# Linear attention with a mixing layer and a gated FFN: q's and k's fp16 parts by one cast and one subtraction, the clamp folded into the product, and new orders of all stages

## The reference

```
x = inv(I - circulant(ricker(width, damp))) @ x        # over channels
t = x as 1024 tokens of 128
a = layernorm(t)
Q, K = elu(a @ Wq.T) + 1, elu(a @ Wk.T) + 1            # 8 heads of 16
V    = a @ Wv.T
S, z = cumsum over tokens of K (x) V, of K
t = t + ((Q . S) / max(Q . z, 1e-6)) @ Wout.T
z = layernorm(t)
g = mean over tokens of gate(z)                        # 8 gates per batch
t = t + layernorm_affine(z + FFN(z)), FFN's weights merged by g
out = t back in x's layout
```

## Time and profile before

| | |
|---|---|
| median of 3 runs | 771.26 us (769.69 to 775.61) |
| profiled execution | 771.21 us, span 769.4 us |
| PE busy | 699.8 us (91%) |
| DVE busy | 670.8 us (87%) |
| ACT busy | 648.9 us (84%) |
| POOL busy | 534.8 us (70%) |
| DMA queue q1 | 82.0 MB, 46.6% of 16 engines' span |
| mean granted clock of PE | 0.968 |

### The profile page before, as it was taken

One profiled execution on the slowest core, in us unless ns is written; L12 is line 12 of the kernel. 1 busy time (PEld: TensorE's weight loads), 2 busy tenths in 40 slices (PEclk: granted clock), 3 DMA queues, 4 the chain that ended last, 5 costly groups with the idle time before them and its releaser, 6 DMA issues. The chain is left out here.

```text
span 769.4 us, 41594 instructions
## 1 busy us (share of the span) xinstructions
PE 699.8 (91%) x13218; PEld 549.2 (71%) x13218; DVE 670.8 (87%) x2615; ACT 648.9 (84%) x1860; POOL 534.8 (70%) x1167
## 2 busy tenths in 40 slices
PE   4897989999999999999999999768999998999993
PEld 2566767777777777777777777656777787777772
DVE  5697889999999999999999999657889877898983
ACT  3687989999999999999999999645888885888883
POOL 3788889999999999999999999420333331333333
PEclk9999989999999999999999999699999999999997
DMA  5558575665666666666665664510122220222221
GB/s 145 112 94 145 104 131 125 132 141 133 129 147 136 134 140 142 138 136 140 134 145 131 139 144 99 82 37 23 43 84 82 82 69 15 84 82 82 82 82 68
DMA packets 202343, 82.60 MB, mean 107 GB/s; under 512 B 176076, under 2 KB 189551, under 8 KB 202232
## 3 DMA queue, kind: packets, MB, share of 16 engines
q1 hardware_dynamic: 202296, 81.99, 46.6%
HBM read 22.69 MB, written 17.30 MB: 52 GB/s over the span
## 5 line engine op out<-in xcount | busy, mean ns | idle before, releaser
L874 DVE SCALAR_TENSOR_TENSOR scores_lo<-p_a,scores_hi 128x512 f16<-128x512 f32 x256 | 175.8, 687 | 7.1 <-ACT scores_hi L760 3.4
L760 ACT ACTIVATE scores_hi<-p_a 128x512 f16<-128x512 f32 x256 | 161.7, 641 | 11.0 <-PE p_a L601 10.7
L979 POOL CAST qk_parts<-qk_f 128x256 f16<-128x256 f32 x256 | 108.8, 427 | 6.3 <-issue 4.3
L1414 POOL TENSOR_TENSOR ffn_rstd_shift<-ffn_rstd_shift,consts 128x4 f32<-128x4 f32 x32 | 36.6, 1142 | 108.8 <-DVE ffn_rstd_shift L1372 108.8
L989 POOL TENSOR_TENSOR qk_parts<-qk_f,qk_parts 128x128 f16<-128x128 f32 x256 | 103.9, 426 | 0.9
L1350 DVE TENSOR_TENSOR h_lo<-h_f,h_hi 128x512 f16<-128x512 f32 x128 | 95.7, 786 | 0.9 <-ACT h_hi L1252 0.9
L1196 PE MATMUL psb<-merged_W_of_batch,h_hi 128*128 128x128 f16 x512 | 94.1, 220 | 2.2 <-DVE h_lo L1350 1.6
L1241 ACT ACTIVATE h_f<-psb,merged_b_of_batch 128x512 f32<-128x512 f32 x128 | 87.0, 710 | 10.3 <-PE psb L1177 8.6
L1197 PE MATMUL psb<-merged_W_of_batch,h_hi 128*128 128x128 f16 x512 | 93.7, 219 | 0.0
L1198 PE MATMUL psb<-merged_W_of_batch,h_lo 128*128 128x128 f16 x512 | 93.7, 219 | 0.0
L618 PE MATMUL p_o<-v_parts,scores_hi 128*128 128x17 f16 x1024 | 90.4, 171 | 2.0 <-issue 0.2
(11 more groups left out here) (215 smaller groups left out, 2859.4 us busy)
## 6 DMA issues: line engine op xcount, KB each, us to landing
x_f<-in_x SPq DMA_DIRECT2D x32, 256.0 KB, 3.1
t_rows<-t SPq DMA_DIRECT2D x64, 128.0 KB, 2.4
t_back<-t_rows SPq DMA_DIRECT2D x32, 256.0 KB, 2.6
out<-out_tile SPq DMA_DIRECT2D x32, 256.0 KB, 2.0
tv_share<-in_L_ffn_tv_W SPq DMA_DIRECT2D x32, 128.0 KB
qkT_parts<-qk_parts SPq DMA_TRANSPOSE x128, 3.1
zT_hi_lo<-z_parts SPq DMA_TRANSPOSE x128, 2.3
merged_W<-in_L_ffn_W SPq DMA_DIRECT2D x2, 256.0 KB, 4.1
```

Source lines behind the costliest of these rows:

```text
L760: nc.scalar.activation(ah[:, t % 2, cols], p_a[:, cols], ACT.Relu).then_inc(ahi_ready[eo], 1)
L874: nc.vector.scalar_tensor_tensor(al[:, t % 2, cols], p_a[:, cols], 0.0, ah[:, t % 2, cols], ALU.max, ALU.subtract).then_inc(alo_ready[eo], 1)
L979: nc.gpsimd.tensor_copy(dst, src.unsqueeze(2).broadcast_to([P, NH, 2, DH])).then_inc(done, 1)
```

## The change

Three things:

- q's and k's hi parts are written by one cast of 512 elements per partition (each value of q and k twice) and their lo parts by one subtraction of 256, in place of two casts and two subtractions. For that k's columns are laid out as lo, hi, hi, 0 and q's as hi, hi, lo, 0, so that one access pattern with a step of 528 columns reaches both; the tile gets 32 columns more per buffered tile (PKW = 1056). The semaphores qhi_ready and khi_ready become qkhi_ready.
- The clamp of the denominators (a tensor_scalar on DVE) goes. invert takes the reciprocal of the sum in PSUM, and divide becomes one scalar_tensor_tensor: min(1/den, 1/(1e-6 VS)) times the numerators.
- All five order tables are new, in order and in skews. Among the skews: project 0 to 1, gate 13 to 15, turn_z 10 to 14, z_hi 10 to 11, z_lo 10 to 12, normalise 10 to 11, gate_relu 14 to 15, rsqrt1 1 to 0, load_x 3 to 4, invert 5 to 6.

```diff
+PKW = 2 * (NH * 4 * DH + DH)
...
-TENSOR_ORDER = [("state", 3), ("scores", 4), ("turn_out", 6), ("conv", 0), ("values", 5), ("out_project", 6),
-                ("project", 0), ("gate", 13)]
+TENSOR_ORDER = [("gate", 15), ("state", 3), ("project", 1), ("scores", 4), ("conv", 0), ("turn_out", 6),
+                ("values", 5), ("out_project", 6)]
...
-SYNC_ORDER = [("turn_z", 10), ("turn", 2), ("load_x", 3), ("load_tv", 3), ("store", 8)]
+SYNC_ORDER = [("turn_z", 14), ("turn", 2), ("load_x", 4), ("load_tv", 3), ("store", 8)]
...
-                    def denominator(b, t):
+                    def invert(b, t):
                         n = TILES * b + t
                         dve.wait_ge(av_done, n + 1)
-                        nc.vector.tensor_scalar(dn[:, t % 2, 0, :], num[:, :, DH], 1e-6 * VS, None, ALU.max)\
-                            .then_inc(den1, 1)
...
+                        nc.vector.reciprocal(dn[:, t % 2, :], num[:, :, DH]).then_inc(den2, 1)
...
-                        nc.vector.tensor_tensor(o_[:, t % 2, :].rearrange("p (h i) -> p h i", i=DH), num[:, :, 0:DH],
-                                                dn[:, t % 2, 1, :].unsqueeze(2).broadcast_to([P, NH, DH]), ALU.mult)\
+                        nc.vector.scalar_tensor_tensor(o_[:, t % 2, :].rearrange("p (h i) -> p h i", i=DH),
+                                                       dn[:, t % 2, :].unsqueeze(2).broadcast_to([P, NH, DH]),
+                                                       1.0 / (1e-6 * VS), num[:, :, 0:DH], ALU.min, ALU.mult)\
                             .then_inc(o_ready, 1)
...
+                    def parts_of(tile, first, w_step, width):
+
+                        return bass.AP(pkw[:, :, :].tensor, PKW * tile + first,
+                                       [[4 * PKW, P], [w_step, 2], [4 * DH, NH], [1, width]])
...
+                        src = qk[:, t % 4, :].rearrange("p (g i) -> p g i", i=DH)
+                        nc.gpsimd.tensor_copy(parts_of(t % 4, 0, NH * 4 * DH + DH, 2 * DH),
+                                              src.unsqueeze(2).broadcast_to([P, 2 * NH, 2, DH])).then_inc(qkhi_ready, 1)
...
-                        for w in range(2):
-                            src = qk[:, t % 4, w * C:(w + 1) * C].rearrange("p (h i) -> p h i", i=DH)
-                            lo = pk[:, t % 4, w, :, (1 + w) * DH:(2 + w) * DH]
-                            last = nc.gpsimd.tensor_tensor(lo, src, pk[:, t % 4, w, :, 0:DH], ALU.subtract)
-                        last.then_inc(lo_ready, 1)
+                        pool.wait_ge(qkhi_ready, n + 1)
+                        nc.gpsimd.tensor_tensor(parts_of(t % 4, 2 * DH, NH * 4 * DH - 2 * DH, DH),
+                                                qk[:, t % 4, :].rearrange("p (w h i) -> p w h i", w=2, i=DH),
+                                                parts_of(t % 4, DH, NH * 4 * DH, DH), ALU.subtract).then_inc(lo_ready, 1)
```

More of the change, by code:

```diff
@@ L36 @@
 TVW = FO * C // B
+PKW = 2 * (NH * 4 * DH + DH)
 EPS = 1e-5
 BIG = -1.0e30
-TENSOR_ORDER = [("state", 3), ("scores", 4), ("turn_out", 6), ("conv", 0), ("values", 5), ("out_project", 6),
-                ("project", 0), ("gate", 13)]
[L44 to L50, removed]
-SYNC_ORDER = [("turn_z", 10), ("turn", 2), ("load_x", 3), ("load_tv", 3), ("store", 8)]
+TENSOR_ORDER = [("gate", 15), ("state", 3), ("project", 1), ("scores", 4), ("conv", 0), ("turn_out", 6),
+                ("values", 5), ("out_project", 6)]
+SCALAR_ORDER = [("relu_qk", 2), ("split_x", 0), ("tv_hi", 0), ("read_t1", 7), ("normalise", 11), ("gate_relu", 15),
+                ("state_hi", 3), ("exp_qk", 1), ("scores_hi_0", 4), ("copy_out", 6), ("scores_hi_1", 4),
+                ("v_hi", 1)]
+VECTOR_ORDER = [("invert", 6), ("make_qk", 2), ("divide", 6), ("mean_var2", 9), ("stats2", 7), ("state_lo", 3),
+                ("stats1", 0), ("v_lo", 2), ("eps2", 9), ("shift2", 10), ("tv_lo", 0), ("mean_var1", 0),
+                ("scores_lo_0", 4), ("eps1", 0), ("scores_lo_1", 4)]
+GPSIMD_ORDER = [("split_x", 0), ("z_hi", 11), ("qk_hi", 2), ("z_lo", 12), ("qk_lo", 2), ("rsqrt2", 9),
+                ("rsqrt1", 0)]
+SYNC_ORDER = [("turn_z", 14), ("turn", 2), ("load_x", 4), ("load_tv", 3), ("store", 8)]
 FFN_TENSOR_ORDER = [("up_0", 0), ("up_3", 0), ("up_1", 0), ("down_0", 1), ("down_1", 1), ("down_2", 1),
@@ L308, in _ @@
                 def _(pool):
-                    nc.gpsimd.memset(pk[:, :, :, :, :].rearrange("p a b h c -> p (a b h c)").bitcast(F32), 0.0)
+                    nc.gpsimd.memset(pkw[:, :, :].rearrange("p t c -> p (t c)").bitcast(F32), 0.0)
                     nc.gpsimd.memset(w1s[:, :].bitcast(F32), 0.0)
@@ L376, in build @@
             st2 = sb(pa_, "stats2", [P, 4, 16])
[L377 removed]
+            dn = sb(pa_, "inverse_denominators", [P, 2, NH])
             gjunk = sb(pa_, "gate_hidden", [P, P])
@@ new lines, in qk_hi @@
+                    def qk_hi(b, t):
+                        n = TILES * b + t
+                        made, used = (n + 1, n - 3) if isinstance(n, int) else (pool.to_reg(n + 1), pool.to_reg(n - 3))
+                        pool.wait_ge(ones_set, 1)
+                        pool.wait_ge(qk_ready, made)
+                        for i in range(2):
+                            at_least(pool, sc_done[i], used)
+                        src = qk[:, t % 4, :].rearrange("p (g i) -> p g i", i=DH)
+                        nc.gpsimd.tensor_copy(parts_of(t % 4, 0, NH * 4 * DH + DH, 2 * DH),
+                                              src.unsqueeze(2).broadcast_to([P, 2 * NH, 2, DH])).then_inc(qkhi_ready, 1)
@@ L1018, in _ @@
                         "split_x": split_x,
-                        "rsqrt2": rsqrt2, "q_hi": qk_hi(0, qhi_ready), "k_hi": qk_hi(1, khi_ready), "z_hi": z_hi, "z_lo": z_lo})
+                        "rsqrt2": rsqrt2, "qk_hi": qk_hi, "z_hi": z_hi, "z_lo": z_lo})
         with ExitStack() as pb:
```

36 lines of the change are left out of this document (8 added, 28 removed).

## The result

The changed kernel took 829.5 us (median of 4 runs, 827.6 to 832.9) beside 771.4 for the kernel before on the same chip: a ratio of 1.075, 95% interval 1.072 to 1.079. The forecast was slower, at 796 us, with 818 as the upper end of the range. The direction was right, and the time was 33 us above the forecast. Some executions of a kernel run at a lower clock as a whole; the ratios leave them out, and where a profile is of such a one, its time is given.

What follows compares the result with a forecast made beforehand. SP's issuing (27.7 us per round) was as full as POOL; the changed order would be bound by a ring, 30.1 us per round. 14 rounds at +1.6 give +22.4, the last gate +2: 771.2 + 24.4, said as 796 us, range 757 to 818.

Steps and rivals of the forecast that it cites:

- the ring: Loop normalise, POOL, SP, landing, gate, scores, ScalarE, next normalise: closes in three slots, 3.62 us per slot, above SP's list.
- the landing: z's DMA transpose, from issue on SP to the gate: 2.3 us plus handing over, 2.40 us.
- Rival 1: SP stays the bound, z's transposes never make anyone wait: 758 us, chance 18%.
- the passage: One trip from normalise to the normalise three slots later: 10.86 us, perhaps off by 0.3 us.
- Sum 10.86 for three slots: Six links added from normalise to the next normalise: 10.86 us, 3.62 per slot, 29.0 per round.
- two passages per round: Two trips around the ring and two slots on SP fill a round: 29.9 us, 30.1 with 0.2 for unpriced links.
- the forecast has 22.4: First stage, 84 to 484 us: 14 rounds, each 1.6 us longer, +22.4 us.
- TensorE's link: From gate to scores_hi_0: gate 0.17, project 0.49, state and mask 0.48, scores 0.39, with handing over 1.63 us.
- the forecast has 2: The last gate comes one slot later: 0 to 3.6 us, taken as +2.
- four hand-overs: Handing over from engine to engine in the ring: 0.10 us each, between 0 and 0.2, without a row.
- Rival 3: Waits at the slot's head leave TensorE idle and lower its clock: 18 to 36 us more, 814 to 832 us, 10%.

Runs made afterwards that it cites:

- run 6: The changed kernel with six needless 128x128 matmuls per slot ahead of TensorE's wait for z's transposition at the gate: 812.7 us.
- Run 1: The changed kernel with turn_z at skew 13 in place of 14, so z's transposition is issued one slot earlier: 759.55 us, ratio 0.983.
- run 7: The changed kernel with a needless GpSimd subtraction ahead of z_lo's in each slot: 850.8 us alone, 832.2 us together with the six matmuls of run 6.
- run 3: The changed kernel with the five order lists of the kernel before, the shared cast at k_hi's place: 783.2 us, ratio 1.009.
- run 4: As run 3, but with the shared cast at q_hi's place, ahead of z_lo: 776.8 us, ratio 1.013.

## Why the prediction was right, and where it failed

Right: that the new order makes it slower and the new operations do not; the ring and each of its links; where TensorE and SP would wait; POOL below 85% with a cast of 0.62 and a subtraction of 0.67 to 0.70 us; the clamp gone, and the product, now 280 ns, no dearer than in the earlier trace rows (283); the landing, 2.51 us from turn_z to the gate. By the forecast's estimate from the Trainium skill (page "VectorE: DVE Perf Modes", section "The three transpose paths", 1309 ns for a 128x128 DMA transpose), the ring would hardly have cost anything; the trace disagrees, with 2.3 us from issue to landing for 128x256. Rival 1, SP as the bound, was refuted by one slot alone: with turn_z at 13, where SP waits for nothing, its time of 758 us is nearly what was measured (759.6).

**The step that failed is the size of the passage.** "Sum 10.86 for three slots" was 11.70, or 11.50 without SP's 0.20, which with the forecast's two passages per round makes 31.4 to 31.8 us for the 30.1; measured were 31.6 in the changed kernel's rounds at full clock and 31.73 in run 6. Over the 14 rounds run 6 takes 448.6 us (30.46 to 479.08), 37 more than the kernel before, where the forecast has 22.4: 15 us.

TensorE's link was the most off, 1.63 for 2.04. From gate to state it took 0.46 us, booked at 0.17, a third of project's columns, where the forecast's own have 0.32 (247.79 to 248.11). From project to mask it took 0.59 for 0.49. The rest was as forecast. Run 1, whose gate does not wait for the DMA, shows what is left of this without a wait:

```profile
219.89 0.22 PE L657 MATMUL p_m<-zT_hi_lo,gate_hi 128*128 x1
...
220.15 0.30 PE L574 MATMUL p_s<-v_parts,qk_parts 128*64 128x17 f16 x8
...
220.53 0.32 PE L556 MATMUL p_in<-w_in_hi,x_hi 128*128 128x384 f16 x1
...
221.11 0.30 PE L594 MATMUL p_a<-mask_bf,ident_bf 64*64 64x256 bf16 x4
221.24 0.39 PE L603 MATMUL p_a<-qkT_parts 64*64 64x128 f16 x16
```

From gate to scores it is 1.35 us, against 1.14 forecast and 1.54 in the passage. So half of the 0.40 was too low a price for this order, wait or no wait, and the other half is between gate and state: 0.26 us here, and 0.43 to 0.50 in all 29 slots from 200 to 428 us in which the changed kernel's weight loads stood still before the gate. (The 28.4 us that the waits put down to "issue" at the gate's weight load are the same standstills as the 22.4 of the product for the DMA, and not added to them.) That state's own waits and registers are worked off beside matmuls when TensorE has some queued, and bare behind a wait, is my reading and was not tried by itself.

**The second is the low clock, booked at 0** in the sum and as a rival of 10% that replaced the forecast, not as a consequence of it. Run 6 measures it at 17 us by the medians, 15 if each is taken beside the kernel before on its own chip, and 13 by the 14 rounds (461.8 less 448.6). It comes with the ring, since the ring is what makes TensorE stand; with turn_z at 13 the mean clock was 0.98. The Trainium skill, page "TensorE: Matmul & The Clock Gate", Part 1, has waits for DMAs between matmuls as a cause of a clock that swings; the stretches of run 6 agree (a wait of 1.73 us for the DMA, then 0.51 for 7 us).

The profiled spans add up: 24.4 us forecast, 15 for the passage, 13 for the clock, and 4 outside these rounds, where 6.3 were measured and the forecast has 2, make the 57 from 769.4 to 826.3, as far as run 6 stands for the changed kernel at full clock. Neither of the first two misses alone would have left the range: 811 and 809 us.

**The bounds.** The range took the passage as known within 0.3 us, and four hand-overs between 0 and 0.2. It had no term for what passes between two stages on one engine. Rival 3 had the right time, 814 to 832, by luck: for a sum of parts that was not the measured one (18 to 36 us of clock on a round of 30.1).

**Not settled.** The 0.25 us per round of run 7, and why the executions of run 3 scatter up to 792 us, with a low clock in every round of the profiled one, and those of run 4 only up to 783, though the quickest of both take 774 to 775.

## What to carry to other kernels

In a pipeline of skewed stages, follow each transfer from the first wait to the stage that feeds it again and count the slots that it gets; divide the sum of its links by that count, and compare with the fullest engine. A ring that is just over is repaired by one slot at its transfer, here 70 us by one number. Price its links by what they take behind a wait, and when the ring makes TensorE stand, add the low clock to the forecast and don't set it beside it.

## What was not expected of the hardware

- Needless work made the kernel faster: six matmuls of 128x128 per slot, ahead of a wait, 829.5 to 812.7 us with the clock from 0.93 to 0.99.
- A DMA transpose costs SP nearly the same whatever its size: 1.17 us for 128x256, 1.19 for 128x512 and 1.23 for qkT_parts (128x1024), and the landing of 128x512 was 2.4 us against 2.3. Merging two saves SP one issue of 1.17 us and makes the landing 0.1 us later.
- On GpSimd a cast of 512 elements per partition took 0.57 us from start to start (277.17 to 277.74), against 0.36 for 256 in the earlier trace rows: not double.
